# Alternating the gate and the up products of every unit between two PSUM banks

## What is computed

```
x = x + (x @ W_base.T + b_base + 2 * sum_e cond[b,e] * (x @ As[e].T) @ Bs[e].T)
shared = (gelu(x @ sh_gate) * (x @ sh_up)) @ sh_down
expert_e = (gelu(x @ ex_gate[e]) * (x @ ex_up[e])) @ ex_down[e]
x = x + shared + sum over the two largest cond[b,:] of weight * expert_e
```

## Time and profile before

| what | value |
|---|---|
| time, median of 3 runs | 146.32 us (146.22 to 146.63) |
| profiled execution, span from first to last instruction | 144.9 us |
| profiled execution, its own time | not recorded apart from the span; the median of the runs is 1.4 us above the span |
| TensorE matmul, busy | 138.4 us (96%), 807 matmuls |
| VectorE, busy | 77.0 us (53%) |
| ScalarE, busy | 73.5 us (51%) |
| GpSimd, busy | 29.7 us (21%) |
| granted TensorE clock, mean | 1.000 |
| shared stage | about 16.3 to 52.8 us |
| expert stage | about 52.8 to 142 us, one unit in 2.72 us in the steady part |

### The profile page before, as it was taken

The page is one execution under the profiler, slowest core; times in us unless marked ns, Lnnn a source line. Parts: engine busy times, 40 slices in busy tenths (PEclk is TensorE's granted clock), DMA queues, the critical chain, the costliest instruction groups (busy, mean ns, idle before and its releaser), DMA issues.

```text
span 144.9 us, 3121 instructions
## 1 busy us (share of the span) xinstructions
PE 138.4 (96%) x807; PEld 116.2 (80%) x808; DVE 77.0 (53%) x129; ACT 73.5 (51%) x129; POOL 29.7 (21%) x39
## 2 busy tenths in 40 slices
PE   7899999999899899999999999999999999999991
PEld 6567876767678678889889889889889889889891
DVE  2799899998997986233233233233233233233220
ACT  3235979659759564544344344344344344344340
POOL 2027799831332211011011011011011011010000
PEclk9999999999999999999999999999999999999999
DMA  3997867991000000000000000000000000000001
GB/s 67 286 342 266 295 226 243 264 291 29 0 0 0 0 0 0 5 18 0 18 18 0 18 18 0 18 18 1 18 17 1 18 17 2 18 16 2 18 15 26
DMA packets 10101, 9.44 MB, mean 65 GB/s; under 512 B 1904, under 2 KB 6768, under 8 KB 10096
## 3 DMA queue, kind: packets, MB, share of 16 engines
q1 hardware_dynamic: 9776, 9.31, 21.3%
q10 hardware_dynamic: 320, 0.07, 0.2%
HBM read 8.32 MB, written 1.05 MB: 65 GB/s over the span
## 4 chain that ended last, share of the span: by engine, by line
PE 83%; DVE 5%; ACT 5%; DMA 2%; issue 2%; SPq 0%; DVEq 0%
PE bank L684 20%; PE bank L666 10%; PE bank L668 10%; PE bank L667 10%; PE bank L675 10%; PE bank L623 3%; PE bank L609 3%; PE bank L607 3%; PE bank L608 3%; PE bank L560 3%; DMA xn<-in_x_dram 2%; PE bank L624 2%; PE bank L625 2%; DVE hT_lo L472 2%; PE bank L554 2%
## 5 line engine op out<-in xcount | busy, mean ns | idle before, releaser
L464 DVE SCALAR_TENSOR_TENSOR work<-bank,wgt,work 128x512 f32<-128x512 f32 x32 | 24.0, 751 | 48.1 <-PE bank L668 26.0
L281 ACT ACTIVATE work<-bank 128x512 f32<-128x512 f32 x48 | 28.7, 598 | 39.6 <-PE bank L668 32.0
L684 PE MATMUL bank<-wexd,hT 128*128 x256 | 33.8, 275 | 0.0
L684 PEld LDWEIGHTS bank<-wexd,hT 128*128 128x128 f32 x256 | 31.1, 192 | 0.0
L666 PE MATMUL bank<-wex,xst 128*128 x64 | 27.8, 434 | 0.0
L295 ACT COPY hT<-bank 128x512 f32<-128x512 f32 x32 | 18.8, 586 | 16.6 <-PE bank L675 16.6
L668 PE MATMUL bank<-wex,xst 128*128 x64 | 25.1, 393 | 0.0
L667 PE MATMUL bank<-wex,xst 128*128 x64 | 25.0, 391 | 0.0
L223 POOL CAST xst<-x1s 128x256 fp32r (+1 forms) x16 | 7.3, 462 | 71.1 <-PE bank L668 71.0
L675 PE MATMUL bank<-ident,work 128*128 128x128 f32 x128 | 19.1, 272 | 0.0
L675 PEld LDWEIGHTS bank<-ident,work 128*128 128x128 f32 x128 | 15.8, 139 | 4.1
(11 more groups left out here) (80 smaller groups left out, 135.1 us busy)
## 6 DMA issues: line engine op xcount, KB each, us to landing
raw_ex<-n_L_cond_skill_gate_dram SPq DMA_DIRECT2D x8, 256.0 KB, 3.1
raw_ex<-in_L_cond_skill_up_dram SPq DMA_DIRECT2D x8, 256.0 KB, 4.1
xn<-in_x_dram SPq DMA_DIRECT2D x4, 256.0 KB, 4.2
out_dram<-xT SPq DMA_DIRECT2D x16, 64.0 KB, 1.5
raw_sh<-_L_cond_shared_gate_dram SPq DMA_DIRECT2D x1, 256.0 KB, 4.5
raw_sh<-in_L_cond_shared_up_dram SPq DMA_DIRECT2D x1, 256.0 KB, 5.1
raw_shd<-_L_cond_shared_down_dram SPq DMA_DIRECT2D x1, 256.0 KB, 5.8
b_nat<-in_L_cond_Bs_dram SPq DMA_DIRECT2D x1, 64.0 KB, 2.4
```

Source lines behind the costliest of these rows:

```text
L281: act.activation(gelu_sb[q], gate_ps[q][:, :], ACT.Gelu_apprx_tanh).then_inc(gelu_done, 1)
L464: dve.scalar_tensor_tensor(h_sb[q], up_ps[q][:, :], wgt[:, k, bass.ds(b, 1)], gelu_sb[q], ALU.mult, ALU.mult).then_inc(h_done, 1)
L684: mm = pe.matmul(bank[4 + j][:, 0:H], hT[:, q, c * P:(c + 1) * P], wexd[:, bass.ds(expert + c * H, H)], start=(k == 0 and c == 0), stop=(k ...
```

## The change

In both `gate_up_shared` and `gate_up_expert` the six matmuls are the same, with the same operands and banks, but issued gate, up, gate, up, gate, up. `gate_done` is raised by the fifth matmul, where it was the third; `up_done` stays on the sixth. The wait for `ex_ulo` in the first expert unit moves from before the first up matmul to before the last.

```
-                for first, ps, done in ((G_HI, gate_ps[q], gate_done), (U_HI, up_ps[q], up_done)):
-                    w_hi = wsh[:, first + c * P:first + (c + 1) * P]
-                    w_lo = wsh[:, first + I + c * P:first + I + (c + 1) * P]
-                    pe.matmul(ps[:, :], w_hi, x1_hi(g), start=True, stop=False)
-                    pe.matmul(ps[:, :], w_hi, x1_lo(g), start=False, stop=False)
-                    pe.matmul(ps[:, :], w_lo, x1_hi(g), start=False, stop=True).then_inc(done, 1)
+                gate, up = gate_ps[q], up_ps[q]
...
+                pe.matmul(gate[:, :], g_hi, x1_hi(g), start=True, stop=False)
+                pe.matmul(up[:, :], u_hi, x1_hi(g), start=True, stop=False)
+                pe.matmul(gate[:, :], g_hi, x1_lo(g), start=False, stop=False)
+                pe.matmul(up[:, :], u_hi, x1_lo(g), start=False, stop=False)
+                pe.matmul(gate[:, :], g_lo, x1_hi(g), start=False, stop=True).then_inc(gate_done, 1)
+                pe.matmul(up[:, :], u_lo, x1_hi(g), start=False, stop=True).then_inc(up_done, 1)
...
+                pe.matmul(gate[:, :], xst[:, j, 0, :], g_hi, start=True, stop=False)
+                pe.matmul(up[:, :], xst[:, j, 0, :], u_hi, start=True, stop=False)
+                pe.matmul(gate[:, :], xst[:, j, 1, :], g_hi, start=False, stop=False)
+                pe.matmul(up[:, :], xst[:, j, 1, :], u_hi, start=False, stop=False)
+                pe.matmul(gate[:, :], xst[:, j, 0, :], g_lo, start=False, stop=True).then_inc(gate_done, 1)
+                if first_unit:
+                    pe.wait_ge(ex_ulo, E)
+                pe.matmul(up[:, :], xst[:, j, 0, :], u_lo, start=False, stop=True).then_inc(up_done, 1)
```

More of the change, by code:

```diff
@@ L603, in gate_up_shared @@
                     pe.wait_ge(h_done, t - 1)
-                for first, ps, done in ((G_HI, gate_ps[q], gate_done), (U_HI, up_ps[q], up_done)):
-                    w_hi = wsh[:, first + c * P:first + (c + 1) * P]
-                    w_lo = wsh[:, first + I + c * P:first + I + (c + 1) * P]
-                    pe.matmul(ps[:, :], w_hi, x1_hi(g), start=True, stop=False)
-                    pe.matmul(ps[:, :], w_hi, x1_lo(g), start=False, stop=False)
-                    pe.matmul(ps[:, :], w_lo, x1_hi(g), start=False, stop=True).then_inc(done, 1)
+                gate, up = gate_ps[q], up_ps[q]
+                g_hi = wsh[:, G_HI + c * P:G_HI + (c + 1) * P]
+                g_lo = wsh[:, G_HI + I + c * P:G_HI + I + (c + 1) * P]
+                u_hi = wsh[:, U_HI + c * P:U_HI + (c + 1) * P]
+                u_lo = wsh[:, U_HI + I + c * P:U_HI + I + (c + 1) * P]
+                pe.matmul(gate[:, :], g_hi, x1_hi(g), start=True, stop=False)
[4 more added lines that the diff above has]
+                pe.matmul(up[:, :], u_lo, x1_hi(g), start=False, stop=True).then_inc(up_done, 1)
             def down_shared(g, c):
@@ L660, in gate_up_expert @@
                 w0 = pe.snap(expert * (GU // DN))
[L661 to L668, removed]
+                gate, up = gate_ps[q], up_ps[q]
+                g_hi = wex[:, bass.ds(w0 + G_HI, I)]
+                g_lo = wex[:, bass.ds(w0 + (G_HI + I), I)]
+                u_hi = wex[:, bass.ds(w0 + U_HI, I)]
+                u_lo = wex[:, bass.ds(w0 + (U_HI + I), I)]
+                pe.matmul(gate[:, :], xst[:, j, 0, :], g_hi, start=True, stop=False)
[6 more added lines that the diff above has]
+                pe.matmul(up[:, :], xst[:, j, 0, :], u_lo, start=False, stop=True).then_inc(up_done, 1)
             def h_transposes(n, q):
```

## The result

The changed kernel takes 149.57 us (median; 149.26 to 150.57) against 146.38 us: a ratio of 1.0231, 95% interval 1.0195 to 1.0268. It is 3.2 us slower, where I forecast 147.7 us and a range of 146.9 to 149.3. The profiled execution is the slowest of the four, 150.57 us with a span of 148.8 us; 1.1 us of that lies in the setup, which the change doesn't touch (the first shared matmul starts at 17.41 us, before at 16.30). So I count positions from that first matmul.

What follows compares the result with a forecast made beforehand. TensorE bounds the kernel (matmuls in flight 96% of the span), with VectorE near its limit in the shared loop. Terms 0 + 0.8 + 0 + 0.2 + 0.4 = 1.4 us gave 147.7 us, range 146.9 to 149.3.

Steps and rivals of the forecast that it cites:

- The rate: TensorE's gate and up matmuls: bank alternation leaves each step at 0.23 us, cost 0.
- The gate result later by two steps: In each of 48 units the gate result comes 0.46 us later; cost 0 in the steady expert stage.
- Rival 3: Gate and up matmuls: the bank matters after all, each step 0.22 us, 144.8 us in all; chance 0.06.
- The first shared unit: Start of the shared stage: VectorE's delayed line 478 still gets in before GpSimd's cast, cost 0, but close.
- rival 1: First shared unit: GpSimd goes before VectorE's line 478, costing 1.3 us, 149.0 us in all; chance 0.20.
- the sign that I gave for it: First shared unit: line 478 ending at 19.56 as before means the forecast, some 0.6 us later means rival 1.
- The head of the first pass: First h of the shared loop's first pass: VectorE waited for its own lo, gelu in time, cost 0.
- The heads of passes 2 and 3: First h of these shared-loop passes: no slack behind the gelu, 0.39 and 0.46 us, together 0.8 (0.85).
- The ring: Shared loop: h, lo, lo, h, sum, TensorE, gate, gelu, h; one gate-to-gelu step per pass, 0.8 us together.
- Into the expert stage: Before the first expert unit: GpSimd's later line 233 runs into VectorE's last line 478, 0.2 us (0 to 0.5).
- The end: After the last unit no matmuls cover h, so the last transposes and all behind shift 0.37 us (0.4).
- the small terms: The forecast's minor costs, whose bounds let its main case reach from 147.1 to 148.3 us.

Runs made afterwards that it cites:

- e3: The changed kernel with every unit in the order up, up, gate, gate, gate, up: 149.51 us, ratio 1.0202.
- e2: The kernel before with the new order in the expert stage only: 146.95 us, ratio 1.0027.
- e4: The changed kernel with the old order in the first shared unit alone: 148.12 us, ratio 1.0101.
- e1: The kernel before with the new order in the shared stage only: 149.21 us, ratio 1.0195.
- e5: The kernel before with the new order in the first shared unit alone: 148.38 us, ratio 1.0122.
- f2: The kernel before with the previous group's last hi and lo ahead of the first gelu and h, in groups 2 and 3 only: 146.07 us, ratio 0.9979.
- e9: The changed kernel with GpSimd's last-group cast of line 217 made to wait for VectorE's first line 478: 148.27 us, ratio 1.0116.
- e6: The kernel before with the new order only in the first unit of groups 1 to 3: 147.67 us, ratio 1.0086.
- f1: The kernel before with the previous group's last hi and lo ahead of the first gelu and h, in all three passes: 147.10 us, ratio 1.0048.
- e8: The changed kernel with every unit in the order gate, up, gate, gate, up, up: 148.24 us, ratio 1.0118, in two clusters.

## Why the prediction was wrong

In the order of its own steps; the sizes are differences of positions in the traces above.

- **The rate: right.** 0.23 us a step behind the first of a unit, and 2.72 us a unit, with every step between two banks; e3 has the same time with fewer changes. Rival 3 is out.
- **The gate result later by two steps: right**, and in the steady expert stage it costs nothing, as forecast (e2).
- **The first shared unit: the step that failed.** I had 0 there, "but close", and the true term is 1.35 us (group 0, 8.56 less 7.21; the changed kernel less e4 at the first expert matmul, 38.99 less 37.63, gives 1.36). My start for line 478 came out 0.01 us behind GpSimd's cast, and I let VectorE win by the one row at 31.15, in which VectorE had been the first by 0.03 us. In the four traces with the first unit delayed by two steps (the changed kernel, e1, e3, e5) VectorE came 0.12 to 0.31 us behind the cast. Two things were off: h follows the gelu's end by 0.10 us (18.85 + 0.60, h at 19.55), where I took 0.03, which is the step from ScalarE's line 288 to VectorE's lo (21.83 to 21.86 before) but in no trace the one from a gelu to its h (the shortest is 0.08, in f2); and GpSimd's place against TensorE's varies by 0.2 us from run to run. The first was enough by itself: in e3 the cast stood where it had stood before (2.64 us after the first shared matmul, before 2.66), and VectorE came 0.12 us behind it. With a margin of 0.01 us such a term is an open choice of two, and should have had even chances or worse; I gave rival 1 one in five. Its price, 1.3 us, was right, but the sign that I gave for it was not: line 478 ended 0.32 us later and not 0.6, since the lo behind it paid.
- **The head of the first pass: 0 forecast, 0.46 measured** (e4, 9.87 against 9.41). I took the gelu as there in time, because the row at 25.71 names VectorE's own lo as the last to end. But at this head h starts 0.63 us after the gelu's end in the kernel before,

```profile
24.48 0.60 ACT L281 ACTIVATE work<-bank 128x512 f32<-128x512 f32 x1
```

(until 25.08, h at 25.71), in the changed kernel (27.99, h at 28.62) and, to 0.01 us, in each of e1 to e9. In e4 the lo ended where it had ended before, 9.13 us after the first shared matmul, and h came 0.46 us later, as its gelu did. So this gelu set the first h already and had no slack. At the heads of passes 2 and 3 the step from the gelu's end to h is 0.30 to 0.32 us; why it is twice that at the first is open.
- **The heads of passes 2 and 3: 0.85 forecast, 0.56 measured** (0.29 and 0.27 in e4). The ring is right, as e6 shows with 0.47 and 0.42. What I missed gives some back: with ScalarE's list later, GpSimd's line 233 no longer goes ahead of the third lo. Before, that lo took 1.63 us and TensorE waited for it:

```profile
40.45 1.29 POOL L233 TENSOR_TENSOR wex<-raw_ex,wex  x1 [2.66 <-ACT wex L302]
...
40.66 1.63 DVE L472 TENSOR_TENSOR hT_lo<-work,hT_hi 128x512 fp32r<-128x512 f32 x1
```

Now line 478 is the one that is held. In the changed kernel:

```profile
43.90 0.68 DVE L472 TENSOR_TENSOR hT_lo<-work,hT_hi 128x512 fp32r<-128x512 f32 x1
44.01 1.72 POOL L233 TENSOR_TENSOR wex<-raw_ex,wex  x1 [2.98 <-ACT wex L302]
...
44.50 1.77 DVE L478 TENSOR_TENSOR wex<-raw_ex,wex  x1
```

From the fourth unit to the next head TensorE takes 2.15 us (44.04 to 46.19), before 2.34 (40.81 to 43.15): 0.19 us less, and 0.46 less 0.19 is the measured 0.27.

- **Into the expert stage: 0.2 forecast, 0.13 measured. The end: 0.37 forecast, 0.38 measured** (0.36 in e2, which has it alone).
- **The sum:** 1.35 + 0.46 + 0.56 + 0.13 + 0.38 = 2.9 us, against the 1.4 forecast. Of the miss of 1.5 us the first unit is 1.35. The first head's 0.46, which I had at 0, is nearly made up by the 0.29 and 0.07 that I had too much at the other heads and into the expert stage; that these cancel is luck. The result lies beyond rival 1 (149.0) and just beyond the range's end at 149.3, which held rival 1 without room for the small terms on top of it.

As to the Trainium skill, page "SBUF — State Buffer", section "Who interferes with whom": its rule, that whoever issues first holds the ports, decided the first unit the way I had not taken, and e9 agrees with it: with VectorE let in first, 1.09 of the 1.35 us are gone.

## What to carry to other kernels

A matmul that ends an accumulation is a signal. When one reorders matmuls, look first at which of them raises a semaphore, how much later it comes, and whether the engines behind it have slack in each stage: the same edit cost nothing in 31 expert units and 2.5 us in the shared stage. Where the traces show two engines that exclude each other, and a delay makes their starts nearly equal, the order may flip, and the price is then of the size of the other's instruction (here paid one instruction later, at the lo) and not of the delay; give both ways a like chance, and let the range hold the dear one with the small terms added. And the engine that a row names as the last to end is no proof that another had slack: compare the step from each of the two in several places or kernels, and the one that stays the same is the one that sets the start.

## What was not expected of the hardware

- A turn between VectorE and GpSimd that flipped cost 1.35 us, with a delay of 0.46 us as its cause, and one wait on GpSimd, which makes it start later, took 1.3 us off the changed kernel (e9; 1.1 us by the traces).
- A VectorE instruction with both inputs in SBUF that GpSimd held ended 0.53 to 0.56 us after GpSimd's wherever the traces list the two by themselves (18.61 + 0.95 against 19.01 before; 22.70 against 22.15 after); h and the sum, which take one input from PSUM, kept their 0.68 us beside GpSimd (h at 18.00 before, the sum in f1).
- With half the delay (e8) the same kernel ran in two clusters, 147.15 and 149.4 us in the mean. What decides between them was not traced.
